# First attention of an early-fusion model: next group's rows, queries, two position images and keys moved beside the units of the group before

## The reference

```
q = grouped_proj(x, Wq) * SCALE          # 12 heads of 64, from 4 groups of 48 features
k = grouped_proj(x, Wk, bk); v = grouped_proj(x, Wv, bv)      # v: 12 heads of 16
content_score = einsum(q + r_w_bias * SCALE, k)
pos_score     = rel_shift(einsum(q + r_r_bias * SCALE, r_head))   # 203 relative positions
attn = softmax(content_score + pos_score) @ v
out  = layernorm(x + attn @ Wo + bo) * gamma + beta;   h = h + out
```

## Time and profile before

| | |
|---|---|
| three runs | 1708.67, 1708.69, 1711.43 us |
| the profiled execution | 1715.82 us, its span 1714.1 us |
| mean granted clock of TensorE | 0.903 |
| busy, share of the span | PE 84%, DVE 39%, ACT 39%, POOL 23% |
| first attention | from about 33 to 309 us of the span |

### The profile page before, as it was taken

One profiled execution on the slowest core, in us unless ns is written; L12 is line 12 of the kernel. 1 busy time (PEld: TensorE's weight loads), 2 busy tenths in 40 slices (PEclk: granted clock), 3 DMA queues, 4 the chain that ended last, 5 costly groups with the idle time before them and its releaser, 6 DMA issues.

```text
span 1714.1 us, 31773 instructions
## 1 busy us (share of the span) xinstructions
PE 1434.5 (84%) x10300; PEld 1046.3 (61%) x10300; DVE 670.6 (39%) x2083; ACT 677.0 (39%) x2261; POOL 385.7 (23%) x464
## 2 busy tenths in 40 slices
PE   6888888684775877888899899699999999889994
PEld 4555555641221445666667899566765776779994
DVE  5555655611101176444423622333442423551113
ACT  1666766320000133777743112154553632113331
POOL 5212113200000023222200166321220200023441
PEclk8898997587777779999999899799999999989997
DMA  8523423659999600000001576300000110126553
GB/s 218 139 63 82 128 69 82 226 162 343 293 290 293 190 11 1 1 0 0 0 1 30 139 211 193 108 1 1 0 0 0 63 65 1 30 77 201 180 176 103
DMA packets 94435, 178.67 MB, mean 104 GB/s; under 512 B 35578, under 2 KB 54168, under 8 KB 92704
## 3 DMA queue, kind: packets, MB, share of 16 engines
q1 hardware_dynamic: 80144, 130.65, 26.3%
q10 hardware_dynamic: 7056, 30.67, 5.7%
q0 software_dynamic: 7136, 16.10, 3.0%
HBM read 150.39 MB, written 26.99 MB: 103 GB/s over the span
## 4 chain that ended last, share of the span: by engine, by line
PE 52%; issue 17%; DMA 11%; DVE 10%; ACT 5%; SPq 3%; POOL 1%; DVEq 0%; ACTq 0%; POOLq 0%
PE bank L1774 12%; DMA WM<-in_fc 8%; PE bank L2250 6%; PE bank L2236 4%; PE bank L1864 4%; PE bank L1876 3%; PE bank L1893 3%; PE bank L1903 3%; PE bank L2240 3%; PE bank L1953 2%; SPq L223 2%; ACT ON L1575 2%; PE bank L1946 1%; DMA pos_scratch<-AREA 1%; DVE MXU L921 1%
## 5 line engine op out<-in xcount | busy, mean ns | idle before, releaser
L1774 PE MATMUL bank<-XT,AREA 96*128 96x408 f32 (+1 forms) x640 | 239.5, 533 | 33.1 <-ACT XT L1529 15.8
L1774 PEld LDWEIGHTS bank<-XT,AREA 96*128 96x128 f32 (+1 forms) x640 | 122.0, 196 | 139.7 <-issue 100.5
L1864 PE MATMUL bank<-KZ,QT 128*102 128x102 f32 x1152 | 143.7, 265 | 16.4 <-ACT ON L1575 6.7
L651 POOL TENSOR_TENSOR RS<-VE,expo 102x4 f32<-102x4 f32 (+1 forms) x53 | 53.1, 1002 | 422.8 <-DVE VE L866 327.4
L1864 PEld LDWEIGHTS bank<-KZ,QT 128*102 128x102 f32 x1152 | 124.8, 178 | 30.6 <-issue 14.0
L667 POOL TENSOR_TENSOR PB<-PB,RCU 102x306 f32<-102x306 f32 x96 | 67.0, 698 | 292.6 <-DVE RCU L927 292.3
L2250 PE MATMUL bank<-WM,KZ 128*128 x660 | 118.2, 327 | 0.0
L2250 PEld LDWEIGHTS bank<-WM,KZ 128*128 128x128 f32 x660 | 105.7, 190 | 0.4
L1556 ACT ACTIVATE KZ<-bank,AREA 128x128 f32<-128x128 f32 x198 | 54.9, 375 | 121.7 <-PE bank L2240 121.7
L1876 PE MATMUL bank<-AREA,OT 128*102 128x192 f32 x384 | 87.9, 342 | 15.4 <-DVE SLOTS L1133 5.4
L1893 PE MATMUL bank<-PT,V 102*32 102x102 f32 (+1 forms) x1152 | 85.6, 269 | 16.7 <-DVE OT L937 13.8
(11 more groups left out here) (335 smaller groups left out, 2764.8 us busy)
## 6 DMA issues: line engine op xcount, KB each, us to landing
AREA<-in_fc SPq DMA_DIRECT2D x10, 1536.0 KB, 24.3
SLOTS<-in_m3w SPq DMA_DIRECT2D x33, 384.0 KB
WM<-in_fc ACTq DMA_DIRECT2D x5, 2304.0 KB, 19.6
WM<-in_fc SPq DMA_DIRECT2D x6, 1536.0 KB, 20.9
AREA<-in_fc ACTq DMA_DIRECT2D x4, 2304.0 KB, 22.0
SLOTS<-in_m1w SPq DMA_DIRECT2D x33, 256.0 KB
AREA<-pos_scratch SPq DMA_DIRECT2D x16, 459.0 KB
pos_scratch<-AREA SPq DMA_DIRECT2D x8, 913.5 KB
```

The costliest lines, as they stand in the source:

```text
L1774: last = pe.matmul(dst, lhsT, rhs, start=n == 0, stop=n == len(pieces) - 1)
L1864: last = pe.matmul(psum[k][0:T, cols(j)], QT[:, tile, cols(bb)], KALL[:, unit % per_tile * (HEADS // per_tile) + tile, cols(bb)], start=Tr ...
```

## The change

Queries, keys, the turned rows and position images 0 and 1 of group g + 1 are made beside the units of group g, in the image banks 6 and 7. Group 0's are made ahead of the loop. The last group is written out after the loop of three.

- Steps: the next group's layer norm begins after unit 2, is applied after 4, kept after 6; at step 6 PE turns the rows; at 7, 8, 9 two query tiles each; at 10 to 15 two pairs each of images 0 and 1; at 19, 20, 21 two key tiles each. ACT's and PE's loops over steps are called with the step (`beside`, `beside_ahead`).
- Query tiles are written once from the bank, as `QR`. DVE makes `QT` from it in steps 16 to 18 with `DQ`, the difference of the biases.
- DVE writes key tiles 1, 3 and 5, ACT 0, 2 and 4 (before DVE had 1 and 4).
- `front`: values, then PE waits for both image banks and for `queries_ready`.
- PE's scores of unit s wait for DVE's addition of unit s − 2 (`scores_taken`), not for ACT's exponentials.
- `finish_0` is split in three parts after units 8, 9 and 10 of the next group (12, 13, 14 of the last group); for the last group they follow it, one behind the other.
- SP waits for `pos_used` in the same way for every image; `pos_used` becomes a mark of its own.

```diff
+TURN_AHEAD, QUERIES_AHEAD, POS_AHEAD, KEYS_AHEAD = 6, (7, 8, 9), (10, 11, 12, 13, 14, 15), (19, 20, 21)
+QUERIES_BACK, VECTOR_KEYS = (16, 17, 18), (1, 3, 5)
...
-                    if bb < 2:
-                        sp.wait_ge(sem["pos_used"], at.now("pos_used"))
-                    else:
-                        sp.wait_ge(sem["pos_used"], at.take("pos_used"))
+                    sp.wait_ge(sem["pos_used"], at.take("pos_used"))
...
-            with at.loop(pool, NG - 1):
-                probabilities((4,))
-                powers(1)
-            probabilities((4, 8))
+            probabilities((2,))
+            with at.loop(pool, NG - 2):
+                probabilities((2, 8))
+            probabilities((4, 12), (8,))
             powers(1)
...
                     ins = tt(p, scores, POS[bb % 2][:, HPU * unit:HPU * unit + HPU, :], ALU.add)
+                    give(ins, "scores_taken")
+                    dve.wait_ge(sem["scores_taken"], at.now("scores_taken"))
                     if unit == UPB - 1:
-                        give(ins, "pos_used")
-                        dve.wait_ge(sem["pos_used"], at.now("pos_used"))
-                    else:
-                        step(ins)
+                        mark("pos_used")
...
                 def between(s):
+                    after = s - (8 if g + 1 < NG else 12)
+                    if g > 0 and 0 <= after < 3:
+                        FINISH[after](g - 1)
                     if g + 1 < NG:
+                        if s in POS_STEPS:
+                            passed(XBANKS, 2)
+                        if s == 2:
+                            begin_a0(g + 1)
                         if s == 4:
-                            begin_a0(g + 1)
+                            turn_a0(g + 1)
                         if s == 6:
-                            turn_a0(g + 1)
-                        if s == 8:
                             keep_a0(g + 1)
...
+                        if s in QUERIES_AHEAD:
+                            queries_ahead(2 * QUERIES_AHEAD.index(s))
...
+                        if s in QUERIES_BACK:
+                            queries_back(2 * QUERIES_BACK.index(s))
+                        if s in KEYS_AHEAD:
+                            keys_ahead(2 * KEYS_AHEAD.index(s))
...
+            def queries_back(first):
+
+                for p in (first, first + 1):
+                    last = ts(QT[:, p, :], QR[:, p, :], DQ[:, p:p + 1], None, ALU.add)
+                if first == 4:
+                    give(last, "queries_ready")
...
-                            pe.wait_ge(sem["exp_ready"], at.take("exp_ready"))
+                            pe.wait_ge(sem[scores_read], at.take(scores_read))
...
+                    beside(s)
+                    if s == TURN_AHEAD:
+                        pe.wait_ge(sem["xn_ready"], at.take("xn_ready"))
+                        turned.extend(turn_group(XN, halves))
+                        fresh.append(True)
+                    if s in QUERIES_AHEAD:
+                        n = 2 * QUERIES_AHEAD.index(s)
+                        if n == 0:
+                            moved(*turned)
+                        q.extend(project(wq0, p6) for p6 in (n, n + 1))
+                    if s in POS_AHEAD:
+                        n = POS_AHEAD.index(s)
+                        if n == 0:
+                            moved(*q[2:4])
+                        if n == 2:
+                            moved(*q[4:6])
+                        pos(n // 3, 2 * (n % 3), 2)
+                    if s in KEYS_AHEAD:
+                        n = 2 * KEYS_AHEAD.index(s)
+                        for p6 in (n, n + 1):
+                            project(wk0, p6)
...
+            at.first_banks()
+            xt()
+            q_moved = [project(wq0, p6) for p6 in range(6)]
+            moved(*q_moved[-2:])
+            pos(0)
+            pos(1)
+            for p6 in range(6):
+                project(wk0, p6)
+            with at.loop(pe, NG - 1):
+                v_moved = front()
+                attention(2, 16, wo0, v_moved, beside_ahead())
+            v_moved = front()
+            attention(2, 16, wo0, v_moved, beside)
```

More of the change, by code:

```diff
@@ L1085, in queries @@
                 if p not in VECTOR_TILES:
[L1086 to L1090, removed]
+                    return passed(XBANKS)
+                k = at.bank(XBANKS)
+                free(ts(QR[:, p, :], full(k)[:, 0:TG], -0.125, rr0[:, p:p + 1], ALU.mult, ALU.add), k)
             def keys(p):
[L1093 to L1095 removed]
+                if p not in VECTOR_KEYS:
+                    return passed(XBANKS)
+                k = at.bank(XBANKS)
                 src = full(k)[:, 0:TG]
@@ L1117, in _ @@
             passed(XBANKS)
-            passed(TBANKS, 6)
+            at.first_banks()
+            passed(XBANKS, 2)
+            for first in (0, 2, 4):
+                queries_ahead(first)
+            passed(XBANKS, 12)
+            dve.wait_ge(sem["pr_ready"], 2)
+            for first in (0, 2, 4):
+                queries_back(first)
+            for first in (0, 2, 4):
+                keys_ahead(first)
             for g in range(NG):
                 at.first_banks()
[L1121 to L1131, removed]
                 values(V, 16, bv0)
@@ L1564, in attention @@
             def attention(pos=None):
-                for s in range(UNITS + 4):
+                for s in range(UNITS + (6 if pos else 4)):
                     if 0 <= s - 4 < UNITS:
@@ L1595, in _ @@
                 free(activation(RT[:, p, :], full(k)[:, 0:NREL], ACT.Copy), k)
[L1596 to L1611, removed]
-                    free(activation(KZ[64:128, 1, p, :], src[64:128], ACT.Identity, bias=bk0[64:128, p:p + 1]), k)
-                def pos_rows(bb, first=0, n=len(POS_PAIRS), banks=XBANKS):
-                    if first == 0:
-                        act.wait_ge(sem["pr_stored"], at.now("pr_ready") * 32 + 32)
-                    for h0, h1 in POS_PAIRS[first:first + n]:
-                        k = at.bank(banks)
-                        src = full(k)[0:T, 0:2 * NREL].rearrange("p (h n) -> p h n", h=2)
-                        free(activation(PR[bb % 2][:, h0:h1 + 1:h1 - h0, 0:NREL], src, ACT.Copy), k)
-                    if first + n == len(POS_PAIRS):
-                        mark("pr_ready")
-                for p in range(4):
-                    queries(p)
-                pos_rows(0, 0, 2, FBANKS)
-                for p in (4, 5):
-                    queries(p)
-                pos_rows(0, 2, 4, FBANKS)
-                pos_rows(1, 0, 6, FBANKS)
-                for p in range(6):
-                    keys(p)
-                attention(pos_rows)
@@ new lines, in queries, with keys @@
+            def queries(p):
+                k = at.bank(XBANKS)
+                if p in VECTOR_TILES:
+                    return passed(k)
+                free(activation(QR[:, p, :], full(k)[:, 0:TG], ACT.Identity, scale=-0.125, bias=rr0[:, p:p + 1]), k)
+            def keys(p):
+                k = at.bank(XBANKS)
+                if p in VECTOR_KEYS:
+                    return passed(k)
+                src = full(k)[:, 0:TG]
+                activation(KZ[0:64, 0, p, :], src[0:64], ACT.Identity, bias=bk0[0:64, p:p + 1])
+                free(activation(KZ[64:128, 1, p, :], src[64:128], ACT.Identity, bias=bk0[64:128, p:p + 1]), k)
@@ new lines, in pos_rows @@
+            def pos_rows(bb, first=0, n=len(POS_PAIRS)):
+                if first == 0:
+                    act.wait_ge(sem["pr_stored"], at.now("pr_ready") * 32 + 32)
+                for h0, h1 in POS_PAIRS[first:first + n]:
+                    k = at.bank(XBANKS)
+                    src = full(k)[0:T, 0:2 * NREL].rearrange("p (h n) -> p h n", h=2)
+                    free(activation(PR[bb % 2][:, h0:h1 + 1:h1 - h0, 0:NREL], src, ACT.Copy), k)
+                if first + n == len(POS_PAIRS):
+                    mark("pr_ready")
@@ L1637, in slot_exponentials @@
+            at.first_banks()
+            turned(XT)
+            for p in range(6):
+                queries(p)
+            pos_rows(0)
+            pos_rows(1)
+            for p in range(6):
+                keys(p)
+            with at.loop(act, NG - 1):
+                attention(beside_ahead)
+            attention(beside)
             def slot_exponentials(dst, src, n, rows):
@@ new lines, in project, with pos @@
+            def project(w, p6):
+                k, p = claim(XBANKS)
+                part, c = p6 // 3, (p6 % 3) * 128
+                return filled(pe.matmul(p[:, 0:TG], w[:, part, c:c + 128], XT[:, part, :],
+                                        start=True, stop=True), k)
+            def pos(bb, first=0, n=len(POS_PAIRS)):
+                for pair in POS_PAIRS[first:first + n]:
+                    k, p = claim(XBANKS)
+                    for j, h in enumerate(pair):
```

(5 more changed lines are left out.)

110 lines of the change are left out of this document (62 added, 48 removed).

## The result

The changed kernel took 1703.13 us (median of 20 runs, 1692.44 to 1717.81) where the kernel before took 1714.35 (20 runs, 1704.70 to 1724.59 but for one). The ratio is 0.9938, with a 95% interval of 0.9919 to 0.9957; the one run of the kernel before that took 6808.62 us counts as slow and is not in the ratio. The medians differ by 11.2 us, the change is faster by 0.6%, and the time is outside my range of 1658 to 1698. A later set of runs (10 against 13) gave a ratio of 0.9983 (0.9961 to 1.0005), with medians of 1709.67 and 1710.63, not to be told from no change. The forecast was 32 us.

A forecast was written before the change was run, and what follows sets the result against it. PE and its issue bound the chain; the units were bound by the round trip between engines. Periods −30.4, group 0's front +1 and group 3 −3 sum to −32.4 us: 1708.7 − 32.4 = 1676 us, range 1658 to 1698.

The forecast's parts named there:

- the drain: From a group's last score to the next group's first: 14.2 us, including 6.3 after the last product with the values.
- the front of group 0: Work before the first score, two banks instead of four: first score some 3 us later, +1 net, ends 0 and +4.
- the last group: Group 3: no image wait, releases by DVE's addition, but group 2's finish on DVE; −3 us, ends −6 and +4.
- The periods: First score to next group's first score, groups 0 to 2: 55 us each instead of 65.1, saving 30.4.
- The units: Steps up to a group's last score: 15.4 with images 2 and 3, 3.0 turn, 9.3 queries, 12.8 images 0 and 1.
- Turn and queries: Units 6 to 9: 3.0 us for the unit with the turn, 3.1 each for three with query projections.
- the spare 1.4 to 2.0: DVE's free time per unit in us, said to cover each part of finish and layer norm, on average.
- The additions: QT from QR on DVE in the drain: two may delay the output copy by 1.3 us.
- The POOL term: Last scaling slowed beside DVE's additions: 0.77 us per period, 2.3 over three; taken as nothing, kept for the range.
- the image wait: Image 0's wait at group starts goes: DVE's quarter of 9.8 us in group 0, −3.3 in group 3.
- rival 3: Slower, chance 0.07: query, turn and key tiles in series through two image banks; period 67.4, 1718 us.
- rival 1: Less than half comes, chance 0.22: DVE's order makes units 2 to 10 DVE-bound and lengthens the drain; period 61, 1694 us.

The follow-up runs named there:

- the run shows in which the delay moved with it: Changed kernel with rebuilt queries one step later, four front banks, group 2's norm at steps 1 to 3, groups 0 and 1's at 11 to 13; ratio 0.9855.
- the run with the old release: Changed kernel, but TensorE's next score of a bank again waits for ScalarE's exponentials, not VectorE's addition; median 1706.75 us, ratio 0.9957.
- all three edits, again: Second run of the changed kernel with rebuilt queries one step later, four front banks, group 2's norm at steps 1 to 3; 1690.91 us, ratio 0.9854.
- the first pair: First traces of the kernel before and the changed kernel: first score at 57.07 and 62.90 us, attention's end at 308.79 and 295.40.
- the second pair: Second traces of the kernel before and the changed kernel, both unchanged: first score at 50.83 and 63.70 us, attention's end at 303.64 and 302.70.
- the three repairs: Changed kernel with rebuilt queries one step later, four banks in group 0's front, group 2's norm at steps 1 to 3; two runs, 1684.2 and 1690.91 us.
- the run with the queries later: Changed kernel with the rebuilt queries made at steps 17, 18 and 19 instead of 16, 17 and 18; median 1704.74 us, ratio 0.9940.

## Why the prediction was wrong, step by step

Three terms of the sum were mis-sized, the drain, the front of group 0 and the last group, and the sum has no term for TensorE's clock, which fell in other places from trace to trace.

**The periods were right to a quarter.** I forecast 55 us each and −30.4; they took 56.3, 57.9 and 58.0, −23.2. The units hold: I summed 15.4 + 3.0 + 9.3 + 12.8 and 0.3, 40.8; the three windows are 39.72, 41.28 and 41.36, 122.4 in all, as forecast to 0.1. In that, two terms cancel. Turn and queries are cheaper, 11.4 instead of 12.3 in group 0. The norm's parts, for which I relied on "the spare 1.4 to 2.0" of VectorE, are not hidden in groups 1 and 2: 41.3 − 39.7 = 1.6 us each. VectorE's mean load left room; its order did not, since TensorE waits for the next copy or addition. That the norm is the cause, the run shows in which the delay moved with it.

**The drain was mis-sized,** 14.2 against 16.6: three times 2.4, all that is missing from the periods. I had seen it as a round trip of two banks; it is TensorE's own work, 14.8 of 16.6 us. The keys cost 4.65 (shown by leaving them out) where I summed 1.46 + 1.27 + 0.73 = 3.5 and a part of a pair before it. The additions, whose possible delay of 1.3 us I named and left out of the sum, cost 0.76, in the half of the drain up to the last product with the values. The rows of the changed kernel place the rest:

```profile
169.95 0.38 PE L1939 MATMUL bank<-PT,V 102*32 102x102 f32 x6
```

Up to there the drain takes 169.95 − 160.50 = 9.45 us, where I had 6.75 + 1.2 = 7.95. Without the 0.76 that leaves 1.9 where I put 1.2 for the last images and the first two keys: half of them was to fall into waits, and little did. From there to the next score it is 7.15 instead of 6.3. The POOL term at nothing was right: the changed kernel's last scaling took 0.69 us with two of the additions beside it.

```profile
163.97 0.69 POOL L664 TENSOR_TENSOR ON<-ON,RCU 102x306 f32<-102x306 f32 x1 [0.60 <-DVE RCU L923]
```

By the rule of the shared port in the Trainium skill (Perfetto Trace Analysis, Optimizing Scalar/DVE Operations) it could have slipped, as it did beside a 768-column addition; beside these additions it did not.

**The front of group 0 was the first large miss.** I took +3 for the first score and gave 2 back for the image wait; but the period of 65.1 already held that wait, so it was counted twice. The size was wrong too. I costed the keys in two banks, and left out the images, which go through the same two: +4.0 us; and the keys took 7.1 us at full clock (51.66 to 58.80, in the run with the old release) against 5.0 with four banks: +2.1 instead of 1.6. From the first query product to the first score the front is 16.5 us before at full clock, 19.1 to 20.7 in four of the five kernels with four banks, and 26.4 at best with two; so two banks cost some 6 us. Of the 2.6 us between 16.5 and 19.1 over half is the clock, low while the queries were made: they took 3.00 + 1.64 = 4.6 us in the second trace of the kernel before (the first two rows) and 6.04 with all three edits, again (the third).

```profile
34.31 3.00 PE L1946 MATMUL bank<-XT,AREA 96*128 96x408 f32 x8 [0.83 <-ACT XT L1527]
...
38.23 1.64 PE L1946 MATMUL bank<-XT,AREA 96*128 96x408 f32 x4
```

```profile
34.93 6.04 PE L1993 MATMUL bank<-XT,AREA 96*128 96x408 f32 x12 [0.69 <-ACT XT L1557]
```

The additions with the order on VectorE are thus left with about 1, the two waits of half a microsecond. At like clock, then, the change costs the front some 7 us (an estimate, 6 + 1); the first pair's 5.8 is less because the front before was itself slow, the second pair's 12.9 more because there it was not. On top of it comes the low clock, up to 33.2 us (below). The ends that I gave, 0 and +4, did not hold it. The rule that independent products should rotate through banks (the Trainium skill, Perfetto Trace Analysis, Matmuls) stood beside rival 3, the slower one; for the images of the front the rows agree, 9.3 against 5.3 us. In the units, which took the 122.4 us of the sum, no such loss shows.

**The last group was the second:** −3 forecast, +4.0 and +2.3 measured. The image wait went as I said (scores of units 1 and 2 are 3.48 us apart instead of 6.09, −2.6 for a forecast −3.3). VectorE no longer waits for a DMA at the line of the addition, 9.8 us before; all but 0.4 us of its idle time there now ends with TensorE (line 911 in the changed kernel, us and times):

```profile
  PE bank L1910: 38.4, 36
```

The early release brought nothing, as the run without it shows. The norm cost 7.1 us where I had "at most 5.6", part of it to be covered. At steps 12 to 14 its parts hold up the last units, and the tail behind them ran at 0.50 to 0.75 in all seven traces. From the tails above, some 3 of the 7.1 are the low clock (an estimate: 18.9 to 19.2 against 16.0 to 16.3); that the late norm brings it on was not shown, since it came with the norm early too, in two of four.

Sum of the misses in the pair of traces: periods 7.2, front 5.8 − 1 = 4.8, last group 4.0 + 3 = 7.0, together 19.0: 32.4 − 19.0 = 13.4, the gain of the trace. In the second pair they are 14.3, 11.9 and 5.3, together 31.5, which leaves 0.9; 8.1 of the 14.3 are the two drains at low clock. None of the rivals came true as priced: periods of 56 to 58 are the forecast's own, and where one came to 59 or more the clock had fallen in it. But rival 1's mechanism, VectorE's order, is what takes the 1.6 us in the units and the 0.76 in the drain. I spent the range on the period and gave the two ends of the pipeline, its filling and its emptying, a few microseconds. With the three repairs, which undo a part of each miss, the gain is 27.3 and 23.3 us (1684.2 against 1711.45, 1690.91 against 1714.25).

## What to carry to other kernels

When a loop is turned into a pipeline, cost the first filling and the last emptying as carefully as the period: work placed there has less beside it to hide behind, and every product that now goes through fewer banks counts, not the new ones alone. An engine with idle time on the mean has none for a piece of work placed ahead of the one copy that the full engine waits for; look at what is queued behind it, and put it where TensorE has other work to do. Take a second trace of the kernel before, and compare stage by stage: the part behind the attention alone varied from 1394.5 to 1412.9 us over these traces with the same code, more than the whole gain.

## What was not expected of the hardware

TensorE's granted clock stood at its lower level (1.2 GHz) in stretches of up to some 20 us in which the engine was busy nearly throughout. The front of the run with the queries later is one such: two windows of it,

```profile
42.00:48.00 6.00, 4.64 (x24) 3.40 (x24) 0.65 (x1) 2.53 (x5) 2.34 (x13) 0.73 0.13 34
48.00:67.61 19.61, 19.61 (x56) 11.30 (x54) 6.61 (x14) 7.84 (x16) 0.00 (x0) 0.50 0.56 152
```

show it idle for 1.4 us at the first images (0.74 and 0.62 us, the waits for two banks), then low, and low for 19.6 us in which it never stopped. Of seven fronts with two banks four ended like this, two fell at the keys and one kept full clock; of the changed kernel's five with four banks four ran their images and keys at full clock throughout, and the fifth came back to it within the images. Of the 21 drains behind two-bank fronts six ran in part at the low clock (up to 21.8 us instead of 16.6), of the 15 behind four-bank fronts none. That the gaps of the front bring this on was not shown: the drain has the same code and the same waits in both, and no run changed the clock alone.
